# Selective scan: the last four state products with B move from TensorE matmuls by diag(B) to scaled transposes, and one product with C moves from GpSimd to VectorE

## The reference, cut to what matters

```python
def step(h, inp):
    u_l, d_l, B_l, C_l = inp
    dA = jnp.exp(d_l[..., None] * A)
    dBu = d_l[..., None] * B_l[:, :, None, :] * u_l[..., None]
    h = dA * h + dBu
    y = jnp.sum(h * C_l[:, :, None, :], axis=-1)
    return (h, y)
h0 = jnp.zeros((Bn, 4, Din, N), xs.dtype)
_, ys = jax.lax.scan(step, h0, inputs)
```

## Time and profile before

| | us |
|---|---|
| median of 3 runs (lowest, highest) | 26504.52 (26499.81, 26509.62) |
| the profiled execution's own time | 26506.39 |
| its span, first to last instruction | 26504.6 |
| one scan stage of eight (window of the first) | 2078.70 |

### The profile page before, as it was taken

The page is one execution under the profiler, slowest core; times in us unless marked ns, Lnnn a source line. Parts: engine busy times, 40 slices in busy tenths (PEclk is TensorE's granted clock), DMA queues, the critical chain, the costliest instruction groups (busy, mean ns, idle before and its releaser), DMA issues. The chain is left out here.

```text
span 26504.6 us, 429162 instructions
## 1 busy us (share of the span) xinstructions
PE 23795.5 (90%) x144992; PEld 17289.0 (65%) x144992; DVE 22358.7 (84%) x22384; ACT 21123.1 (80%) x41992; POOL 20337.8 (77%) x13385
## 2 busy tenths in 40 slices
PE   7999879998799987999879998899988999889998
PEld 3588635886368863688636886468854688546885
DVE  6799867998679986799867998679986799867998
ACT  4799757997579975799757997579975799757997
POOL 3699746997369973699736997369973699736997
PEclk8999989999899998999989999899998999989999
DMA  0111101111011110111101111011110111101111
GB/s 9 34 51 51 43 7 35 51 50 43 6 35 51 51 43 6 35 51 51 43 6 35 51 51 43 6 35 51 51 43 5 36 51 51 43 5 36 51 51 43
DMA packets 650118, 986.05 MB, mean 37 GB/s; under 512 B 204448, under 2 KB 221728, under 8 KB 644640
## 3 DMA queue, kind: packets, MB, share of 16 engines
q1 hardware_dynamic: 647904, 957.96, 12.5%
HBM read 890.60 MB, written 67.11 MB: 36 GB/s over the span
## 5 line engine op out<-in xcount | busy, mean ns | idle before, releaser
L1439 DVE TENSOR_TENSOR_SCAN arena<-arena,ps 128x512 f32<-128x512 f32 x12288 | 14605.6, 1258 | 163.3 <-PE ps L1596 129.5
L1833 ACT ACTIVATE arena<-arena 128x512 f32<-128x512 f32 x12288 | 8421.9, 720 | 79.5 <-PE ps L1635 79.1
L2050 POOL TENSOR_TENSOR arena<-arena 128x1536 f32<-128x1536 f32 x2304 | 7976.7, 3474 | 9.1 <-ACT arena L1865 8.8
L1635 PE MATMUL ps<-ident,arena 128*128 128x128 f32 x49152 | 6596.1, 274 | 22.7 <-DVE arena L1451 4.5
L1635 PEld LDWEIGHTS ps<-ident,arena 128*128 128x128 f32 x49152 | 5589.3, 141 | 549.8 <-issue 447.7
L1588 PE MATMUL ps<-arena 128*128 128x128 f32 x24576 | 3186.0, 279 | 366.5 <-DVE arena L1439 366.1
L1588 PEld LDWEIGHTS ps<-arena 128*128 128x128 f32 x24576 | 2925.5, 192 | 672.8 <-DVE arena L1439 474.4
L1596 PE MATMUL ps<-ident,arena 128*128 128x128 f32 x18432 | 2658.2, 275 | 161.5 <-DVE arena L1439 156.2
L1596 PE MATMUL ps<-ident,scaled 128*128 128x128 f32 x18432 | 2622.8, 274 | 78.0 <-DVE arena L1439 76.9
L2050 POOL TENSOR_TENSOR arena<-arena,spare 128x1536 f32<-128x1536 f32 x768 | 2664.5, 3469 | 34.1 <-ACT arena L1865 11.8
L1596 PEld LDWEIGHTS ps<-ident,arena 128*128 128x128 f32 x18432 | 2093.4, 141 | 595.5 <-DVE arena L1439 406.0
(11 more groups left out here) (201 smaller groups left out, 36061.3 us busy)
## 6 DMA issues: line engine op xcount, KB each, us to landing
arena<-rows SPq DMA_DIRECT2D x2304, 256.0 KB, 3.1
spare<-rows SPq DMA_DIRECT2D x768, 256.0 KB, 3.1
arena<-x SPq DMA_DIRECT2D x18, 1536.0 KB, 12.9
x<-arena SPq DMA_DIRECT2D x16, 1536.0 KB, 10.7
arena<-x SPq DMA_DIRECT2D x64, 384.0 KB, 8.5
out<-arena SPq DMA_DIRECT2D x64, 384.0 KB, 3.0
rows<-xd SPq DMA_DIRECT2D x256, 64.0 KB, 1.6
arena<-L_conv_fc_w SPq DMA_DIRECT2D x16, 576.0 KB, 5.3
```

What stands on the lines that cost most here:

```text
L1439: nc.vector.tensor_tensor_scan(flip(states(b, n, t)), flip(states(b, n, t)), flip(bank(b, n, t)), carry[:, k, N2 * n + t:N2 * n + t + 1], ...
L1635: ins = nc.tensor.matmul(m.ps[:, t, j * 128:(j + 1) * 128], states(b, n, t)[:, j * 128:(j + 1) * 128], m.ident[:, :], start=(n == SUMS[t][ ...
L1833: nc.scalar.activation(states(b, n, t), delta[:, b % 2, t, :], ACT.Exp, scale=aneg[:, b // NT, t, n:n + 1]).then_inc(at["da_ready"], 1)
L2050: nc.gpsimd.tensor_tensor(out, out, each, ALU.mult).then_inc(at["hp_ready"], 1)
```

## The change

1. `DIAGONAL`, the `diagonal` steps and their buffers are gone. All 16 states go through `scale` and the transposes of `turn_back`. `POOL_PIECES` gives GpSimd piece 3 of the even and pieces 2, 3 of the odd states: 24 pieces, and 40 for ScalarE. The two `scaled` buffers now alternate over all sixteen states.
2. `POOL_C` has eleven states, (0, 1, 3, 4, 6, 7, 9, 10, 12, 13, 14); VectorE's are 2, 5, 8, 11, 15. SyncE loads eleven rows of C a block.
3. `SUMS` and the written-out lists of all engines are laid out anew. VectorE's now starts the loop body at state 5.

```diff
-POOL_C = (0, 1, 2, 4, 5, 6, 8, 9, 10, 12, 13, 14)
+POOL_C = (0, 1, 3, 4, 6, 7, 9, 10, 12, 13, 14)
 DVE_C = tuple(n for n in range(NS) if n not in POOL_C)
-DIAGONAL = (2, 6, 10, 14)
-SCALED = tuple(n for n in range(NS) if n not in DIAGONAL)
-POOL_PIECES = {0: (3,), 1: (2, 3), 3: (3,), 4: (2, 3), 5: (3,), 7: (2, 3), 8: (2, 3), 9: (3,), 11: (2, 3), 12: (3,), 13: (2, 3), 15: (2, 3)}
-BY_POOL = tuple((n, j) for n in SCALED for j in range(4) if j in POOL_PIECES.get(n, ()))
-BY_ACT = tuple((n, j) for n in SCALED for j in range(4) if j not in POOL_PIECES.get(n, ()))
+POOL_PIECES = {0: (3,), 1: (2, 3), 2: (3,), 3: (2, 3), 4: (3,), 5: (2, 3), 6: (3,), 7: (2, 3), 8: (3,), 9: (2, 3), 10: (3,), 11: (2, 3), 12: (3,), 13: (2, 3), 14: (3,), 15: (2, 3)}
+BY_POOL = tuple((n, j) for n in range(NS) for j in range(4) if j in POOL_PIECES.get(n, ()))
+BY_ACT = tuple((n, j) for n in range(NS) for j in range(4) if j not in POOL_PIECES.get(n, ()))
...
@@ turn_back(b, n, t) on TensorE
-                if n in DIAGONAL:
-                    no = nth(b, n, DIAGONAL)
-                    pe.wait_ge(at["diag_out"], N4 * (no + 1))
-                    pe.wait_ge(at["turn_out"], (N4 + 1) * (b + 1))
-                    for j in range(N4):
-                        ins = nc.tensor.matmul(bank(b, n, t)[:, j * 128:(j + 1) * 128], turned[b % 2][:, j, t * 128:(t + 1) * 128],
-                                               diagonals[no % 2][:, j, :], start=True, stop=True)
-                    ins.then_inc(at["back_mm"], 1)
-                    return
...
                     ins = nc.tensor.transpose(bank(b, n, t)[:, j * 128:(j + 1) * 128],
-                                              scaled[nth(b, n, SCALED) % 2][:, j, t * 128:(t + 1) * 128], m.ident[:, :])
+                                              scaled[(NS * b + n) % 2][:, j, t * 128:(t + 1) * 128], m.ident[:, :])
...
@@ scale(b, n, j) on GpSimd, and alike on ScalarE
-                if nth(b, n, SCALED) > 1:
-                    past, slot = slot_of(b, n)
-                    pool.wait_ge(at["back_mm"], N2 * (NS * past + SCALED[slot] + 1))
+                if NS * b + n > 1:
+                    pool.wait_ge(at["back_mm"], N2 * (NS * b + n - 1))
...
@@ VectorE's list
                 scan(b, 6, 0)
+                correct(ahead, 0)
                 scan(b, 6, 1)
+                times_c(b, 5)
                 scan(b, 6, 2)
...
                 scan(ahead, 4, 0)
+                times_c(ahead, 2)
+                scan(ahead, 4, 1)
+                scan(ahead, 4, 2)
```

More of the change, by code:

```diff
@@ L1930, in _ @@
                 decay(b, 2, 0)
[L1931 to L1945 removed]
+                save(past, 14)
@@ new lines, in _ @@
+                save(past, 15)
+                scale(b, 1, 1)
+                scale(b, 2, 0)
+                high(ahead)
+                decay(b, 2, 1)
+                keep_rows(ahead)
+                scale(b, 2, 1)
+                scale(b, 2, 2)
+                scale(b, 3, 0)
+                decay(b, 2, 2)
+                scale(b, 3, 1)
+                save(b, 0)
+                lift_y(past, 0)
+                decay(b, 3, 0)
+                save(b, 1)
+                decay(b, 3, 1)
@@ new lines, in _ @@
+                decay(b, 3, 2)
+                scale(b, 4, 0)
+                scale(b, 4, 1)
+                give_y(past, 0)
+                decay(b, 4, 0)
+                lift_y(past, 1)
+                decay(b, 4, 1)
+                scale(b, 4, 2)
+                scale(b, 5, 0)
+                decay(b, 4, 2)
+                low_row(ahead)
+                decay(b, 5, 0)
+                save(b, 2)
+                save(b, 3)
+                decay(b, 5, 1)
+                scale(b, 5, 1)
@@ L1946, in _ @@
+                decay(b, 5, 2)
+                decay(b, 6, 0)
+                give_y(past, 1)
                 softplus(ahead, 0, 0)
                 softplus(ahead, 0, 1)
-                save(b, 2)
-                scale(b, 5, 0)
-                scale(b, 5, 1)
-                decay(b, 4, 1)
-                give_y(past, 0)
-                lift_y(past, 1)
-                scale(b, 5, 2)
-                decay(b, 4, 2)
-                decay(b, 5, 0)
-                decay(b, 5, 1)
+                lift_y(past, 2)
@@ L1958, in _ @@
+                scale(b, 6, 0)
                 softplus(ahead, 0, 2)
-                give_y(past, 1)
-                lift_y(past, 2)
-                save(b, 3)
                 save(b, 4)
+                scale(b, 6, 1)
+                scale(b, 6, 2)
                 softplus(ahead, 0, 3)
                 scale(b, 7, 0)
-                decay(b, 5, 2)
+                give_y(past, 2)
+                scale(b, 7, 1)
+                decay(b, 6, 1)
                 softplus(ahead, 0, 4)
-                decay(b, 6, 0)
@@ L1968, in _ @@
[L1968 to L1973 removed]
                 save(b, 5)
[L1975 removed]
                 decay(b, 6, 2)
                 decay(b, 7, 0)
[L1978 to L1979 removed]
+                scale(b, 8, 0)
                 decay(b, 7, 1)
[L1981 removed]
@@ new lines, in _ @@
+                softplus(ahead, 1, 0)
+                scale(b, 8, 2)
+                scale(b, 9, 0)
+                decay(b, 8, 2)
+                decay(b, 9, 0)
+                decay(b, 9, 1)
+                scale(b, 9, 1)
+                save(b, 7)
+                scale(b, 10, 0)
+                softplus(ahead, 1, 1)
+                scale(b, 10, 1)
+                softplus(ahead, 1, 2)
+                softplus(ahead, 1, 3)
+                scale(b, 10, 2)
+                softplus(ahead, 1, 4)
@@ L1996, in _ @@
+                decay(b, 9, 2)
+                save(b, 8)
+                decay(b, 10, 0)
+                scale(b, 11, 0)
+                scale(b, 11, 1)
+                decay(b, 10, 1)
+                save(b, 9)
+                decay(b, 10, 2)
                 softplus(ahead, 2, 0)
                 softplus(ahead, 2, 1)
-                save(b, 8)
+                decay(b, 11, 0)
+                decay(b, 11, 1)
+                scale(b, 12, 0)
+                decay(b, 11, 2)
+                scale(b, 12, 1)
@@ L2027, in _ @@
-                take_turned(ahead, 0)
+                scale(b, 13, 0)
+                scale(b, 13, 1)
+                save(b, 10)
+                scale(b, 14, 0)
+                save(b, 11)
+                scale(b, 14, 1)
         @block.gpsimd
```

361 lines of the change are left out of this document (141 added, 220 removed).

## The result

| | us |
|---|---|
| before, median of 4 runs (lowest, highest) | 26505.65 (26499.81, 26509.62) |
| after, median of 4 runs (lowest, highest) | 27210.88 (27184.20, 27224.02) |
| ratio after / before (95% interval) | 1.0265 (1.0251 to 1.0278) |
| after, span of the profiled execution | 27222.3 |
| forecast (range) | 26930 (26870 to 27080) |

What follows compares the result with a forecast made beforehand. VectorE's instruction stream was taken to bound the scan stages: 256 blocks x 1.65 us = +422 us on 26506.4, other engines hidden, new waits zero, giving 26928, stated as 26930 us with a few us for small waits; range 26870 to 27080 us.

Steps and rivals of the forecast that it cites:

- The bound: In the scan stages VectorE's instruction stream sets the time: 99.3% busy, 65.01 us a block, 32 blocks a stage.
- VectorE, +1.65 us a block: One more product with C on VectorE, covered by nothing: block from 65.01 to 66.66 us, +422 us over 256 blocks.
- the lower end: Best the new lists can do: lose the 0.37 us a block not at VectorE's fastest spacing, -95 us.
- TensorE, ScalarE, GpSimd: Per block: TensorE -5.5 us, to about 57 of 66.66; ScalarE +0.86, at most 65.87; GpSimd -0.66, at most 64.35.
- All other engines have at least 0.8 us to spare: Per block of 66.66 us, every engine but VectorE has this room, more than before.
- ScalarE's clump at state 6: Thirteen instructions between decays of tiles 0 and 1; decay (6,1) ends by S + 9.80, wanted at S + 10.44.
- GpSimd's piece of state 10: Stands behind two products with C; ready by S' + 7.5, scan (10,0) begins at S' + 12.8: ample.
- the first rival: Waits in the new order, ScalarE late at state 6: with 0.5 us a block, 27056 us; chance 0.2.
- TensorE's clock, chance 0.02: Rival: lighter-loaded TensorE loses its 2.4 GHz clock in the scan stage; at mean 0.80, about 28100 us; chance 0.02.
- the new waits: Waits inside VectorE's list from the new order: taken as zero; one of 1.0 us a block would be +256 us.
- The row: Scan-stage window of the kernel before: granted clock 1.00 with TensorE 95.9% busy, read as 1.00 throughout despite short rests.
- The range: 26870 to 27080 us: forecast plus waits up to 0.6 us a block; below, part of the 0.37 us a block.

Runs made afterwards that it cites:

- filling all three places: Kernel after with the transposes of turn_back (8, 2), (9, 2) and (11, 2) each done twice: 26926.49 us, ratio to before 1.0152.
- Four times over: Kernel after with the four transposes of turn_back (11, 2) done four times over, as useless work ahead of the rest: 27179.04 us, ratio to before 1.0249.
- two variants: Kernel after with turn(ahead, -1) moved behind turn_back(b, 12, 2), 26959.21 us; kernel after with the transposes of turn_back (11, 2) done twice, 26937.07 us.

## Why the prediction was wrong, point by point

**The bound.** Right as far as the runs show it. VectorE's instruction stream fills the 65.01 us, one more product lengthens the block by 1.47, and in the undisturbed blocks after it is dense too, 66.37 busy of 66.37. A dense list isn't proof that it leads alone: in the kernel after, shortening it gained nothing. No run shortens it in the kernel before.

**VectorE, +1.65 us a block.** The mechanism was right, and the size a little high. Five products a block stand 1.65 us each in the trace, scans stay at 1.17. The undisturbed block grew by 1.44 (66.46 - 65.02), the kernel before with one product moved by 1.47. Of the 0.37 us that weren't at fastest spacing, which I kept in the sum and named only as the lower end, about 0.2 went. Over 256 blocks that is 369 to 376 us instead of 422.

**TensorE, ScalarE, GpSimd.** The sum for TensorE was read from its weight loads, and there it holds: they fall from 53.5 us a block (1711.14 us in the 32 blocks of the stage) to 47.8, by 5.7 where 5.5 were forecast. Its matmul rows fell by 2.9 us only, from 62.3 to 59.4, so it is 90% busy in an undisturbed block and not 86%. "All other engines have at least 0.8 us to spare" doesn't hold as a statement on chains. Taking some 1.1 us a block out of VectorE gained nothing, 1.5 out of ScalarE nothing, both together 0.2 us. A list that is busy 65.9 of 66.4 us and makes round trips to TensorE can be as long as the block. It cost nothing here, since VectorE has the same length.

**What is late next.** I looked at ScalarE's clump at state 6 with a margin of 0.6 us for the decay of (6, 1), and at GpSimd's piece of state 10. In the kernel after, neither makes VectorE wait: the undisturbed blocks have no idle time. The wait that came stands at state 13, with ScalarE's decay as its last releaser, as I had written for the first rival. But the decay itself waited for TensorE, and only in blocks with the low clock.

**TensorE's clock, chance 0.02, and the new waits, put at nothing.** This is the step that failed: the term for waits in the sum was zero, and it measured 1.16 us a block, some 300 us, by way of a rival that I had given 0.02. I weighed the clock by its mean over a block: "It decides only below 57/66.66 = 0.855 on average". The mean never came near that. It is 0.97 in a disturbed block and 0.98 in the stage. But TensorE's list is in order, and a stretch of 3.4 us at 1.2 GHz ahead of a decay with little slack puts 1.57 us into the block, even though TensorE has 7 us free in it. The free time lies elsewhere. The evidence that I gave against it, "I see no long rest", was taken from the trace of before, while the lists already told of a new one. On ScalarE the last `softplus` step of tile 2 moved from behind the decay of (10, 0) to behind that of (12, 0), while on TensorE `turn(ahead, -1)` stayed by the products of state 11. I never asked of each TensorE instruction how long it would be held. The price was right in kind (four transposes 0.85 instead of 0.44; the 20 transposes of `add_up` 3.96 instead of 2.35), and only its use was wrong. The row itself was misread too: the clock isn't "at 1.00 throughout the window" of the earlier trace rows. The 1.00 is a mean over 2078.70 us, and the 3.4 us at 0.50 of the earlier trace rows lie inside it. The Trainium skill's page "TensorE: Matmul & The Clock Gate", section "A second HAM failure mode: psum-queue depth-cycling", had spoken for this rival, with short rests that make the clock swing; I let the row of before outweigh it. The trace after agrees in kind: the clock swings in 195 of 240 blocks, and no rest of TensorE in these blocks is longer than 1.9 us.

That rests bring the clock down, and with it VectorE's waits, is shown: removing the rest (-252 us), doing a little useless work ahead of it (-274 us), filling all three places (no low stretch left in the 240 blocks, -284 us), and making a longer rest in the kernel before (155 blocks with a low stretch where there were none) agree. Four times over (-32 us) doesn't fit its number, since falls came elsewhere. Still open: why one block in five or six escapes with the same rest, what part the lighter load and the kind of TensorE's work have, and which chain stands at 66.15.

**The range.** Its upper end came from waits of up to 0.6 us a block. One stretch as in the earlier trace rows can put off the work behind it by up to 3.4/2 = 1.7 us. An estimate with that in every block would have put the upper end at 26928 + 1.7 x 256, about 27360; it measured 1.57 us, in four blocks of five.

## What to carry to other kernels

Ask of a slower stretch on an engine with spare time where it falls on that engine's in-order list, not what it does to the mean: 3.4 us at half clock cost 1.57 us a block on an engine that was free for 7. When an order is laid out anew, go through each instruction that waits for another engine and has unrelated work queued behind it, and place it where its input is already there. And when one engine is full, taking work from the others gave next to nothing here: the B part, some 5 us less on TensorE, was worth 0.02 to 0.12 us a block.

## What the runs showed of the hardware that I had not expected

- In the kernel after, a rest of 1.87 us was followed by 3.4 us at a granted clock of 0.50 in 170 of 240 blocks, and two rests of 0.8 us some 5 us apart in 25 (34 and 40 in two variants). A rest of 1.2 to 1.7 us in each block of the kernel before never was, in the same 240 blocks. Doing the four transposes ahead of a rest twice kept the clock at 1.00 over a rest of 1.4 us.
- The same sequence with the same rest (1.87 us in both blocks shown) kept the clock once and lost it once: every fifth or sixth block escaped, and blocks 4 and 10 did so in all eight stages.
- Matmuls that compute nothing new can pay: 0.44 us of them a block took 1.0% off the kernel.
- VectorE's price for a product over three tiles, 1.65 us by its starts, was 1.44 to 1.47 us net for the block: of the 0.37 us that the old list had beyond its fastest spacing, some 0.2 were gone.
